# Scores by float32 products in four groups of 32 array columns, and outputs stored by accumulating transfers

## The chip, the core and the metric

The kernel runs on one core of one Trainium2 chip. The metric is the device time of one execution in microseconds; the median of three runs is given. The engines are TensorE (matmuls), VectorE, ScalarE, GpSimd and SP, which issues transfers. TensorE reads its weights and its moving operand from SBUF and writes PSUM; transfers run on 16 DMA engines, whichever engine issues them.

## What is computed

```python
q = cond @ Wq.T + bq                       # (2, 512), as 16 heads of 32
k = x @ Wk.T + bk;  v = x @ Wv.T + bv      # x: (2, 2048, 512)
scores = einsum('bhqd,bhkd->bhqk', q / sqrt(32), k)[:, :, 0, :]
attn = clip(scores, 0.0, 1.0)              # one weight per row of x and head
context = attn[..., None] * v
out = x + context.reshape(2, 2048, 512) @ Wo.T + bo
```

All is float32. There is one query per batch element, so the scores of a batch element are x times a 512x16 matrix `a` (Wk folded with the query), plus a constant `c`.

## The kernel before

**Layout.** x lies transposed (features on partitions) and is cut into four superblocks s = 0 to 3 of 1024 rows of x. Superblocks 0 and 1 belong to the first batch element, 2 and 3 to the second. A superblock is a 512x1024 matrix, in four quadrants Q11, Q12, Q21, Q22 of 256 features by 512 rows, each kept as 128 partitions x 1024 (two contraction tiles of 512 columns). One 512-KB transfer loads or stores a quadrant.

**Products.** Each of the two large products (values v, outputs) is a 2x2 block product done in the Strassen-Winograd way with 7 block products: the kinds B11, B21, B22 are quadrants of the operand and T1, T2, T3, T4 are sums of quadrants (T3 replaces Q12 in place). Each operand is split in two float32r parts: ScalarE's `hi` casts it to `form_hi`, VectorE's `lo` subtracts and writes `form_lo`. A block product is 12 matmuls of 128x512: high x high, high x low and low x high, for two contraction tiles and two output tiles. `done[kind]` counts them. ScalarE copies results out of PSUM (`copy_b11`, `copy_u2`, `copy_u3`, `copy_out21`), VectorE adds the rest (`add_out11`, `add_out22`, `add_out12`).

**Phases.** The work runs in phases, values and outputs of the superblocks in turn: V0 (by hand, the opening), V1, O0, V2, O1, V3, O2, O3. They are numbered 0 to 7. The order of every engine is written out by hand, call by call, and engines meet only at semaphores. Engines run in order, so a call that waits holds up all that stands behind it on its engine. `made(kind, phase)` counts an operand's versions.

**Scores.** For each superblock `scores(s, 0)` and `scores(s, 1)` multiply the quadrants' operands already split for the values with the weights `a_for_hi` and `a_for_lo`: 2 x 8 matmuls of 128x512. The first 64 array columns carry the high part of `a`, the other 64 the rest, each head in 4 copies. So ScalarE copies the result (`copy_scores`), SP swaps the halves of the partitions by two transfers (`swap_scores`), VectorE adds them (`sum_scores`), ScalarE applies bias and ReLU (`relu_scores`), and VectorE's `context` takes the minimum with 1 and multiplies by v. The score products hold `form_hi` of the kinds B11, B21, T3 and B22: the next `hi` of these waits for `score_done`.

**The weights of the scores** come up in the opening: `rows(q_rows...)` is four float32 matmuls of 32 columns x 512 rows into the partitions 0, 32, 64 and 96 on (line 453), then transposes, `scale_q`, `rows(a_rows...)`, ScalarE's `copy_a_rows`, transposes (`turn_score_weights`), VectorE's `fill_a`, `sum_c` and `split_a`.

**x and outputs.** x has one home, `x_raw`. A quadrant of the next superblock is loaded when its old operand has been split. Results of the outputs of superblocks 0 to 2 lie in `work[2]`. GpSimd adds x to them by an accumulating transfer from DRAM (`add_residual`, 12 transfers), and SP stores them afterwards (`store`). The last superblock adds x on VectorE (`add_x`) and is stored in pieces.

## Time and profile before

| what | value |
|---|---|
| median of 3 runs | 184.95 us (184.53 to 186.56) |
| the profiled execution's own time | 185.87 us |
| its span (first to last instruction) | 184.1 us |
| granted TensorE clock, mean | 1.00 |
| TensorE matmuls, busy | 178.1 us, 795 |
| VectorE, busy | 164.5 us, 175 |
| ScalarE, busy | 111.7 us, 150 |
| moved by DMA | 30.24 MB, mean 164 GB/s |

The span is what the page divides; the execution's own time holds 1.8 us more around it. Starts are counted from the span's start. The durations of neighbouring instructions of one engine overlap, above all those of matmuls, so the work of an engine is read from the distance between starts.

### The profile page before, as it was taken

The page shows a single profiled execution, that of the slowest core. Times are in us where ns is not written, and L with a number is a line of the kernel's source. Part 1 is how long each engine was busy: PE and PEld are TensorE (multiplying, and loading weights), DVE is VectorE, ACT ScalarE, POOL GpSimd, SP SyncE. Part 2 cuts the span into 40 slices and gives each one's busy share as a digit, 9 for nine tenths or more (in the row PEclk, how much of TensorE's full clock was granted, in tenths as well). Part 3 has the DMA queues.
Part 4 walks back from the last instruction along what each step waited for, and adds up shares of the span by engine and source line. Part 5 has one row for each costly group of instructions (what it writes and reads, how often), then busy time and mean ns, then how long its engine had stood idle before and what let it go on. Part 6 is the DMA issues. An engine that isn't in the chain of part 4 may idle for free.

```text
span 184.1 us, 2338 instructions
## 1 busy us (share of the span) xinstructions
PE 178.1 (97%) x795; PEld 143.1 (78%) x795; DVE 164.5 (89%) x175; ACT 111.7 (61%) x150; POOL 13.4 (7%) x18
## 2 busy tenths in 40 slices
PE   8999999999899999999999999999999999999990
PEld 2786767888688888888888888888888888878880
DVE  1798469999999997999999999999997999999851
ACT  3568394895776755575587567855466847493200
POOL 6000000000000020211000010121000010111000
PEclk9999999999999999999999999999999999999999
DMA  5999930049220226399788226399720216189786
GB/s 217 347 383 389 395 142 0 12 102 360 103 57 0 57 21 179 49 182 207 215 290 287 58 14 155 91 175 310 227 117 0 57 14 155 62 129 236 201 321 254
DMA packets 9355, 30.24 MB, mean 164 GB/s; under 512 B 1152, under 2 KB 1536, under 8 KB 9216
## 3 DMA queue, kind: packets, MB, share of 16 engines
q1 hardware_dynamic: 7616, 23.81, 35.5%
q0 software_dynamic: 1728, 6.29, 20.6%
q8 instruction: 6, 0.10, 0.2%
q14 instruction: 5, 0.04, 0.1%
HBM read 19.61 MB, written 8.39 MB: 152 GB/s over the span
## 4 chain that ended last, share of the span: by engine, by line
PE 81%; DMA 10%; DVE 3%; SPq 2%; issue 1%; ACT 1%; DVEq 0%
DMA x_raw<-x_t 10%; PE bank_y L350 9%; PE bank_y L352 9%; PE bank_y L354 9%; PE bank_x L350 8%; PE bank_x L354 8%; PE bank_x L352 8%; PE bank_z L354 6%; PE bank_z L352 6%; PE bank_z L350 6%; PE score_bank L412 4%; PE score_bank L413 4%; PE bank_z L467 1%; PE bank_z L466 1%; PE bank_z L465 1%
## 5 line engine op out<-in xcount | busy, mean ns | idle before, releaser
L576 ACT CAST form_hi<-work 128x1024 fp32r<-128x1024 f32 x28 | 29.1, 1051 | 20.8 <-PE score_bank L413 6.6
L832 DVE TENSOR_TENSOR form_lo<-work,form_hi 128x1024 fp32r<-128x1024 f32 (+1 forms) x30 | 35.1, 1185 | 0.9 <-ACT form_hi L576 0.9
L611 ACT ACTIVATE work<-bank_y,const 128x512 f32<-128x512 f32 x30 | 19.8, 686 | 7.9 <-PE bank_y L354 7.6
L817 POOL DMA_DIRECT2D work<-x_t x12 | 10.5, 876 | 153.6 <-DVE work L865 147.8
L350 PE MATMUL bank_x<-form_hi,wo_hi 128*128 128x512 f32 x52 | 20.3, 391 | 0.5 <-issue 0.5
L611 ACT ACTIVATE work<-bank_x,const 128x512 f32<-128x512 f32 x24 | 15.8, 685 | 8.2 <-PE bank_x L354 8.2
L352 PE MATMUL bank_x<-form_lo,wo_hi 128*128 128x512 f32 x52 | 20.2, 389 | 0.0
L354 PE MATMUL bank_x<-form_hi,wo_lo 128*128 128x512 f32 x52 | 20.2, 389 | 0.0
L854 DVE SCALAR_TENSOR_TENSOR work<-relu,work 128x1024 f32<-128x1024 f32 x16 | 19.3, 1220 | 0.3 <-ACT relu L640 0.3
L350 PE MATMUL bank_y<-form_hi,wv_hi 128*128 128x512 f32 x48 | 18.7, 389 | 0.0
L352 PE MATMUL bank_y<-form_lo,wv_hi 128*128 128x512 f32 x48 | 18.7, 389 | 0.0
L354 PE MATMUL bank_y<-form_hi,wv_lo 128*128 128x512 f32 x48 | 18.7, 389 | 0.0
L832 DVE TENSOR_TENSOR form_lo<-x_raw,form_hi 128x1024 fp32r<-128x1024 f32 x15 | 18.2, 1220 | 0.1
L576 ACT CAST form_hi<-x_sum 128x1024 fp32r<-128x1024 f32 x9 | 9.5, 1052 | 8.6 <-DVE x_sum L915 4.6
L865 DVE TENSOR_TENSOR work<-bank_z,work 128x1024 f32<-128x1024 f32 x12 | 14.6, 1218 | 0.0
L576 ACT CAST form_hi<-x_raw 128x1024 fp32r<-128x1024 f32 x12 | 12.5, 1048 | 2.8 <-PE bank_y L354 1.3
L832 DVE TENSOR_TENSOR form_lo<-x_sum,form_hi 128x1024 fp32r<-128x1024 f32 x9 | 11.0, 1220 | 2.1 <-ACT form_hi L576 2.1
L412 PE MATMUL score_bank<-form_hi,a_for_hi 128*128 128x512 f32 x32 | 12.6, 393 | 0.2 <-DVE a_for_hi L832 0.2
L413 PE MATMUL score_bank<-form_lo,a_for_lo 128*128 128x512 f32 x32 | 12.5, 389 | 0.0
L350 PEld LDWEIGHTS bank_x<-form_hi,wo_hi 128*128 128x128 f32 x52 | 9.8, 188 | 2.9 <-issue 0.9
L354 PEld LDWEIGHTS bank_x<-form_hi,wo_lo 128*128 128x128 f32 x52 | 9.8, 188 | 2.0
L352 PEld LDWEIGHTS bank_x<-form_lo,wo_hi 128*128 128x128 f32 x52 | 9.8, 188 | 2.0
(139 smaller groups left out, 375.9 us busy)
## 6 DMA issues: line engine op xcount, KB each, us to landing
x_raw<-x_t SPq DMA_DIRECT2D x16, 512.0 KB, 6.4
out_t<-work SPq DMA_DIRECT2D x14, 512.0 KB, 4.1
work<-x_t POOLq DMA_DIRECT2D x12, 512.0 KB, 5.5
score_others<-score_rows SPq DMA_DIRECT2D x16, 128.0 KB, 2.3
work<-first_t SPq DMA_DIRECT2D x2, 512.0 KB, 3.7
work<-wq_t SPq DMA_DIRECT2D x2, 512.0 KB, 8.8
work<-wk_t SPq DMA_DIRECT2D x2, 512.0 KB, 11.1
work<-wo_t SPq DMA_DIRECT2D x1, 1024.0 KB, 7.4
```

Of the source, the lines that this page charges most:

```text
L350: pe.matmul(bank[:, j, :], hi, form_hi[:, kind, k, :], start=k == 0 and not grows, stop=False, skip_group_check=grows)
L352: pe.matmul(bank[:, j, :], hi, form_lo[:, kind, k, :], start=False, stop=False, skip_group_check=grows)
L354: mm = pe.matmul(bank[:, j, :], lo, form_hi[:, kind, k, :], start=False, stop=k == 1, skip_group_check=grows)
L412: pe.matmul(bank, a_for_hi[:, b, at + k, :], form_hi[:, kind, k, :], start=first, stop=False)
L413: mm = pe.matmul(bank, a_for_lo[:, b, at + k, :], form_lo[:, kind, k, :], start=False, stop=last)
L465: pe.matmul(bank, hi, x_hi, start=k == 0 and not grows, stop=False, skip_group_check=grows)
L576: nc.scalar.copy(flat(form_hi, kind), raw(kind, phase)).then_inc(hi_ready[kind], 1)
L611: nc.scalar.activation(result_set(phase)[:, q, j * ROWS:(j + 1) * ROWS], of[:, j, :], ACT.Identity, bias=bias[:, tile:tile + 1], scale=sca ...
L817: pool.dma_start(output_set(s)[:, q, :], x_t[s, q], accum_op=ALU.add).then_inc(residual_added[q], 16)
L832: return nc.vector.tensor_tensor(to, of, hi.bitcast(F32), ALU.subtract)
L854: nc.vector.scalar_tensor_tensor(out=pair(context_set(s), q), in0=relu[:, half:half + 1, :].to_broadcast([P, 2, ROWS]), scalar=1.0, in1=pa ...
L865: nc.vector.tensor_tensor(to, bank[:, :, :], to, ALU.add).then_inc(semaphore, 1)
```

## The change

Three things change, and with them the written order of ScalarE and VectorE.

**Scores.** `scores(s)` reads x itself, unsplit, as float32. The 1024 rows of a superblock are four quarters of 256 rows, and each quarter goes to a group of 32 array columns of its own, that is to 32 partitions of the result: 16 matmuls of 32x256 a superblock (4 contraction tiles by 4 groups). The weights `a_copies` are plain float32, each head in 2 copies. Four ReLUs of 32x256 (`clip_scores`) bring the four groups beside each other on the first 32 partitions, and three transfers (`spread_scores`) copy these to the other partitions. The copy, the swap, the sum and the split of `a` with its zeros are gone. Since T3 stands where Q12 was, superblocks above 0 use `x_t3_ready` and a weight difference for Q22.

**x.** x has two homes, `x_homes[s % 2]`. Superblock 1 is loaded without waiting; superblock s waits for what used s - 2.

**Outputs.** SP copies x to the place of the output, DRAM to DRAM (`copy_x`, four transfers for each of superblocks 0 to 2), and GpSimd stores the results by accumulating transfers onto it.

```diff
-            def scores(s, half):
-                bank, b = score_bank[half][:, :], s // 2
-                wait(pe, score_copied, score_number(s, half) - 1)
...
-                for kind, at in parts:
-                    for k in range(2):
-                        first, last = (kind, k) == (parts[0][0], 0), (kind, k) == (parts[1][0], 1)
-                        pe.matmul(bank, a_for_hi[:, b, at + k, :], form_hi[:, kind, k, :], start=first, stop=False)
-                        mm = pe.matmul(bank, a_for_lo[:, b, at + k, :], form_lo[:, kind, k, :], start=False, stop=last)
+            def scores(s):
+                b = s // 2
+                pe.wait_ge(a_ready, b + 1)
+                for q in range(4):
+                    wait(pe, x_loaded[s % 2][q], loads(q, s))
+                if s > 0:
+                    pe.wait_ge(x_t3_ready, s)
+                wait(pe, clipped_ready, GROUPS * (s - 1))
+                for k in range(KT):
+                    for g in range(GROUPS):
+                        half, rows = g // 2, k % 2 * ROWS + g % 2 * QUARTER
...
+                        mm = pe.matmul(score_psum(s)[g * GROUP:(g + 1) * GROUP, :], a_copies[:, b, form, :], of,
+                                       start=k == 0, stop=k == KT - 1)
+                mm.then_inc(score_done, 1)
...
+            def clip_scores(s):
+                act.wait_ge(score_done, s + 1)
+                act.wait_ge(c_ready, 1)
+                if s > 0:
+                    for ready in context_ready:
+                        act.wait_ge(ready, s)
+                for g in range(GROUPS):
+                    at = slice(g * GROUP, (g + 1) * GROUP)
+                    nc.scalar.activation(relu[0:GROUP, g // 2, g % 2 * QUARTER:(g % 2 + 1) * QUARTER], score_psum(s)[at, :],
+                                         ACT.Relu, bias=c_score[at, b:b + 1]).then_inc(clipped_ready, 1)
...
+            def spread_scores(s):
+                sp.wait_ge(clipped_ready, GROUPS * (s + 1))
+                for g in range(1, GROUPS):
+                    sp.dma_start(relu[g * GROUP:(g + 1) * GROUP, :, :], relu[0:GROUP, :, :]).then_inc(relu_loaded, 16)
+            def copy_x(s):
+                for q in (Q11, Q22, Q21, Q12):
+                    sp.dma_start(out_t[s, q], x_t[s, q]).then_inc(x_copied[s][q], 16)
...
+            load_x(1, Q11)
+            load_x(1, Q12)
             sp.dma_start(wo_raw.rearrange("p t n -> p (t n)"), wo_t.rearrange("p b n -> p (b n)")).then_inc(wo_loaded, 16)
+            load_x(1, Q22)
+            load_x(1, Q21)
+            spread_scores(0)
+            next_x(2)
+            copy_x(0)
+            spread_scores(1)
+            next_x(3)
+            copy_x(1)
+            spread_scores(2)
+            copy_x(2)
+            spread_scores(3)
...
-            def add_residual(s, q, semaphore, count):
+            def store(s, q, semaphore, count):
                 pool.wait_ge(semaphore, count)
-                pool.dma_start(output_set(s)[:, q, :], x_t[s, q], accum_op=ALU.add).then_inc(residual_added[q], 16)
+                pool.wait_ge(x_copied[s][q], 16)
+                pool.dma_start(out_t[s, q], output_set(s)[:, q, :], accum_op=ALU.add).then_inc(accumulated[q], 16)
...
             first_values(Q21, banks[1], 2)
             copy_q_rows()
+            hi(B11, 1)
             hi(T1, 1)
-            first_values(Q12, banks[2], 4)
-            copy_a_rows()
             wo_part(W11, 0)
             wo_part(W12, 1)
             wo_part(W22, 3)
+            first_values(Q12, banks[2], 4)
+            copy_a_rows()
+            hi(B21, 1)
             hi(T2, 1)
```

TensorE at the end of the opening, before (the last products of V0, the first block of scores, then T1 of V1):

```order
L429 MATMUL bank_x<-form_hi,wv_lo 128x512 x4
L412 MATMUL score_bank<-form_hi,a_for_hi 128x512
L413 MATMUL score_bank<-form_lo,a_for_lo 128x512
L412 MATMUL score_bank<-form_hi,a_for_hi 128x512
L413 MATMUL score_bank<-form_lo,a_for_lo 128x512
L412 MATMUL score_bank<-form_hi,a_for_hi 128x512
L413 MATMUL score_bank<-form_lo,a_for_lo 128x512
L412 MATMUL score_bank<-form_hi,a_for_hi 128x512
L413 MATMUL score_bank<-form_lo,a_for_lo 128x512
L350 MATMUL bank_z<-form_hi,wv_hi 128x512
```

and the same place now:

```order
L412 MATMUL bank_x<-form_hi,wv_lo 128x512 x4
L395 MATMUL score_bank<-work,a_copies 32x256 x2
L395 MATMUL score_bank<-x_home,a_copies 32x256 x2
L395 MATMUL score_bank<-work,a_copies 32x256 x2
L395 MATMUL score_bank<-x_home,a_copies 32x256 x10
L327 MATMUL bank_z<-form_hi,wv_hi 128x512
```

Sixteen matmuls stand in one block where two blocks of eight stood, one on each side of T1; those of superblocks above 0 stand ahead of T2 of their values phase.

ScalarE in the opening, from `copy_q_rows` on, before (`wo_hi<-work2` are the three parts of Wo, the second COPY is `copy_a_rows`):

```order
L679 COPY relu<-score_bank0 128x512
L576 CAST form_hi<-x_sum 128x1024
L670 ACTIVATE work0<-bank_z,const 128x512 x2
L683 COPY relu<-score_bank0 128x512
L687 CAST wo_hi<-work2 128x512 x3
L576 CAST form_hi<-x_sum 128x1024
L660 CAST wv_hi<-work1 128x512
```

and now:

```order
L654 COPY relu<-score_bank0 128x512
L553 CAST form_hi<-x_home1 128x1024
L553 CAST form_hi<-x_sum 128x1024
L662 CAST wo_hi<-work2 128x512 x3
L645 ACTIVATE work0<-bank_z,const 128x512 x2
L658 COPY relu<-score_bank0 128x512
L553 CAST form_hi<-x_home1 128x1024
L553 CAST form_hi<-x_sum 128x1024
L635 CAST wv_hi<-work1 128x512
```

The casts of Wo moved ahead of `first_values(Q12)` and of `copy_a_rows`, and the first operands of superblock 1 moved in here.

VectorE in the same stretch, from `fill_a` to the last step of the scores' weights, before:

```order
L1030 TENSOR_REDUCE a_full<-score_bank1 128x128
L1033 TENSOR_TENSOR a_full<-a_full 128x64
L1052 TENSOR_REDUCE c_score<-score_bank0 128x2
L1045 CAST a_for_hi<-a_full 128x6x64
L1045 CAST a_for_lo<-a_full 128x6x64
L832 TENSOR_TENSOR a_for_hi<-a_full,a_for_hi 128x6x64
```

and now:

```order
L988 TENSOR_REDUCE a_full<-score_bank1 128x128
L991 TENSOR_TENSOR a_full<-a_full 128x64
L796 TENSOR_TENSOR wo_lo<-work2,wo_hi 128x512
L1003 TENSOR_REDUCE c_score<-score_bank0 128x2
L796 TENSOR_TENSOR form_lo<-x_home1,form_hi 128x1024
L997 COPY a_copies<-a_full 128x192
```

One copy stands for the split, with a part of Wo and `lo(B21,1)` ahead of it.

## Rows read from the trace of the kernel before

**Rows 1.** The page, part 1: busy us, share of the span, instructions.
```profile
PE 178.1 (97%) x795; PEld 143.1 (78%) x795; DVE 164.5 (89%) x175; ACT 111.7 (61%) x150; POOL 13.4 (7%) x18
```

**Rows 2.** The waits of TensorE: engine, line, releaser, total us, times, longest.
```profile
PE bank_x L350 <- issue: 0.5, 1, 0.5
```

**Rows 3.** Busy time by stretch; then clock, DMA share, GB/s.
```profile
120.00:160.00 40.00, 40.00 (x178) 33.13 (x177) 38.92 (x36) 23.92 (x31) 2.81 (x4) 1.00 0.49 128
```

**Rows 4.** The timeline of TensorE: start, us, engine, line, operation, count.
```profile
165.96 0.39 PE L350 MATMUL bank_x<-form_hi,wo_hi 128*128 128x512 f32 x1
...
168.68 0.39 PE L350 MATMUL bank_y<-form_hi,wo_hi 128*128 128x512 f32 x1
...
172.76 0.28 PE L465 MATMUL bank_z<-form_hi,wo_hi 128*128 128x256 f32 x1
172.87 0.28 PE L466 MATMUL bank_z<-form_lo,wo_hi 128*128 128x256 f32 x1
```

**Rows 5.** The timeline of VectorE from 46.8 us.
```profile
46.80 1.22 DVE L854 SCALAR_TENSOR_TENSOR work<-relu,work 128x1024 f32<-128x1024 f32 x1
47.93 0.68 DVE L841 TENSOR_TENSOR score_rows<-score_rows,score_others 128x512 f32<-128x512 f32 x1
48.53 0.69 DVE L832 TENSOR_TENSOR wo_lo<-work,wo_hi 128x512 fp32r<-128x512 f32 x1
```

**Rows 6.** Groups by form: count, then busy us and mean ns of one.
```profile
L412 PE MATMUL score_bank<-form_hi,a_for_hi 128*128 128x512 f32 x32 | 12.6, 393 | 0.2 <-DVE a_for_hi L832 0.2
...
L640 ACT ACTIVATE relu<-score_rows,c_score 128x512 f32<-128x512 f32 x8 | 5.8, 722 | 1.9 <-DVE score_rows L841 1.9
...
L630 ACT COPY score_rows<-score_bank 128x512 f32<-128x512 f32 x8 | 4.6, 575 | 0.0
```

**Rows 7.** The timeline of TensorE around the query rows (L453).
```profile
14.95 1.07 PE L429 MATMUL bank_y<-form_lo,wv_hi 128*128 128x512 f32 x4
15.95 1.06 PE L453 MATMUL score_bank<-work,const 128*32 128x512 f32 x8
16.95 0.73 PE L429 MATMUL bank_z<-form_hi,wv_hi 128*128 128x512 f32 x2
```

**Rows 8.** Line 453: duration in ns (min, median, max), first and last start.
```profile
L453 PEld LDWEIGHTS score_bank<-work,const x8: 106/108/109, 15.9 to 16.0; 128*32 128x32 f32 x8
L453 PE MATMUL score_bank<-work,const x8: 592/604/617, 15.9 to 16.4; 128*32 128x512 f32 x8
```

**Rows 9.** The timeline of ScalarE, then of TensorE, from 24.5 us.
```profile
24.52 0.59 ACT L683 COPY relu<-score_bank 128x512 f32<-128x512 f32 x1
24.99 1.68 ACT L687 CAST wo_hi<-work 128x512 fp32r<-128x512 f32 x3
...
26.06 0.28 PE L501 MATMUL score_bank<-bk_q,const 128*128 128x8 f32 x2
```

**Rows 10.** DMA issues (KB, median us to landing), and one of SP's timeline.
```profile
work<-x_t POOLq DMA_DIRECT2D x12, 512.0 KB, 5.5
work<-wo_t SPq DMA_DIRECT2D x1, 1024.0 KB, 7.4
...
16.91 0.43 SPq L285 DMA_DIRECT2D work<-wo_t  x1
```

**Rows 11.** The timeline of VectorE from 25.7 us.
```profile
25.71 1.23 DVE L930 TENSOR_TENSOR x_sum<-x_sum,x_raw 128x1024 f32<-128x1024 f32 x1 [0.99 <-DMA x_raw<-x_t]
...
28.60 0.68 DVE L1030 TENSOR_REDUCE a_full<-score_bank 128x128 f32<-128x512 f32 x1
...
29.57 0.36 DVE L1045 CAST a_for_hi<-a_full 128x384 fp32r<-128x384 f32 x1
```

**Rows 12.** The timeline of VectorE and TensorE around 50 us.
```profile
49.13 1.22 DVE L832 TENSOR_TENSOR form_lo<-work,form_hi 128x1024 fp32r<-128x1024 f32 x1
...
50.56 0.47 PE L350 MATMUL bank_x<-form_hi,wo_hi 128*128 128x512 f32 x1 [0.50 <-issue]
```

**Rows 13.** Stores of the output on SP: ns to issue, first and last start.
```profile
L325 SPq DMA_DIRECT2D out_t<-work x3: 588/686/710, 179.3 to 180.6; - x3
```

More of the change, by code:

```diff
@@ L561, in hi @@
                     semaphore, count = {
[L562 to L563 removed]
+                        B11: (x_loaded[s % 2][Q11], loads(Q11, s)), B21: (x_loaded[s % 2][Q21], loads(Q21, s)),
+                        B22: (x_loaded[s % 2][Q22], loads(Q22, s)),
                         T1: (x_t1_ready, s), T2: (x_t2_ready, s), T3: (x_t3_ready, s), T4: (x_t4_ready, s)}[kind]
@@ L569, in hi @@
                     act.wait_ge(semaphore, s + 1)
-                before, s_before = PHASES[phase - 1]
-                if before == VALUES and kind in FIRST_PHASE_KINDS and (kind != B22 or s_before == 0):
-                    act.wait_ge(score_done, score_number(s_before, kind in (T3, B22)) + 1)
+                if phase > 1 or kind not in FIRST_PHASE_KINDS:
+                    wait(act, done[kind], 2 * (phase - 1))
+                elif kind == T3:
+                    act.wait_ge(w21_done, 1)
                 else:
-                    wait(act, done[kind], 2 * (phase - 1))
+                    act.wait_ge(first_done, {B11: 2, B21: 4, B22: 8}[kind])
                 nc.scalar.copy(flat(form_hi, kind), raw(kind, phase)).then_inc(hi_ready[kind], 1)
@@ L1108, in _ @@
             fill_a()
+            wo_part(W12, 1)
             sum_c()
-            split_a(0)
-            wo_part(W12, 1)
+            lo(B21, 1)
+            copy_a(0)
             lo(T2, 1)
+            lo(T3, 1)
             wv_sum_part(S3, 3)
             x_t4(1)
+            lo(B22, 1)
             wo_sum(0)
+            lo(T4, 1)
             wo_sum(1)
-            lo(B11, 1)
-            lo(B21, 1)
-            lo(T4, 1)
             wo_sum(2)
-            lo(T3, 1)
+            wo_sum(3)
             wo_sum_part(S2, 1)
-            lo(B22, 1)
-            wo_sum(3)
-            sum_scores(0, 0)
             wo_sum_part(S1, 0)
+            wo_sum_part(S3, 2)
+            wo_part(W22, 3)
+            add_out11(1)
+            wo_sum_part(S4, 3)
+            copy_a(1)
             context(0, Q11)
-            add_out11(1)
-            context(0, Q21)
-            sum_scores(0, 1)
-            wo_sum_part(S3, 2)
+            context(0, Q12)
             lo(B11, 2)
-            context(0, Q12)
             context_t1(2)
             add_out22(1)
+            context(0, Q21)
             lo(T1, 2)
@@ L1179, in _ @@
             lo(B11, 5)
+            add_out12(3)
             lo(T3, 4)
-            add_out12(3)
+            add_out11(4)
             context_t4(4)
-            add_out11(4)
+            lo(B22, 4)
             lo(T4, 4)
-            lo(B22, 4)
             x_t1(5)
             lo(B21, 5)
-            x_t3(5)
             lo(T1, 5)
@@ L1230, in _ @@
             context_t2(7)
+            context(3, Q21)
+            lo(T2, 7)
+            lo(B21, 7)
             context_t3(7)
-            lo(T2, 7)
             context_t4(7)
```

327 lines of the change are left out of this document (117 added, 210 removed).

## The prediction, written before the changed kernel was run

> **What bounds the kernel now.** I read the page's busy shares first, then the waits by engine, then the busy time by stretch. The reader is to see that TensorE is busy 178.1 of 184.1 us [rows 1], that its longest wait is 0.5 us [rows 2], and that in a stretch such as 120 to 160 us it is busy all 40 us, with the granted clock at 1.00, the higher of its two levels (2.4 GHz) [rows 3]. VectorE stands close behind (38.9 of the 40 us). Busy shares of matmuls overlap, so I take the work from the distance between starts: twelve products from 165.96 to 168.68 us are 2.72 us, 0.2266 us for 512 columns, and a 256-column one is 0.119 us [rows 4]. VectorE's distances are 1.13 us for 128x1024 and 0.60 us for 128x512 [rows 5]. So the end is set by the number of matmuls, and what the change takes from TensorE comes off the span, if the other engines follow.
>
> **What goes from TensorE.** 64 score products, 32 with the high parts [rows 6] and 32 with the low, at 0.2266 us: **-14.5 us**.
>
> **What comes.** 64 float32 matmuls of 32 array columns by 256 rows, 16 per superblock. The trace has a near relative: the query rows, four float32 matmuls of 32 columns by 512 rows, written into four different groups of 32 columns, each with a moving operand of its own [rows 7, 8]. They are recorded as 8 matmuls, two passes each. The first start at 15.95 us, the last at 16.4 us, and each lasts 0.60 us: so the four groups run at the same time, and a pass over 512 rows takes 0.45 us, twice the 0.2266 us of an fp32r product. With 256 rows I take twice 0.119 = 0.233 us (rounding). A superblock has four contraction tiles of two passes, 8 rounds: 1.87 us. The switch costs extra on both sides: the product group ahead began at 14.95 us and four of its matmuls are 0.91 us, so without any switch the next would have begun at 15.86 us; two rounds of 0.45 us later would be 16.76 us, but the next group starts at 16.95 us and its first matmul is 0.11 us late because its weights load only then. That is 0.09 + 0.10 + 0.11 = 0.30 us. A block is then 2.17 us, four are **+8.7 us**. Both sides: below, 8 rounds with no switch, 1.8 us a block (7.2 in all); above, the weight loads stand open in each round (rival A), 3.0 us a block (12.1 in all). I take 8.7 because the row nearest to it is the same form of instruction.
>
> **The opening.** Here the new ScalarE order costs something. TensorE's rows of a need the copy of a_rows (L683); before it is finished at 25.1 us and TensorE turns to it at 26.06 us without a wait [rows 9]. After the change the three casts of wo stand ahead of first_values(Q12) and of that copy. They wait for wo_t, issued at 16.91 us, 7.4 us to landing: at 24.3 us, and at the latest at 24.99 us, where before they begin without a wait [rows 9, 10]. From 24.5 us: casts 1.65 us, two activations 1.15 us, copy 0.6 us, done at about 27.9 us. TensorE stands in front of its transposes for 1.8 us. It comes to scores(0) at 30.5 + 1.8 = 32.3 us, where they now start at 30.72 us after 0.2 us of waiting for the split of a [rows 6]: **+1.6 us** (from 0 if wo lands much earlier, to 2.1). VectorE's side is no later: x_t2(1) cannot start before x arrives at 25.7 us [rows 11], both before and after, since all loads go through one queue in nearly the same order; from its start at 25.7 us two sums and a wo part lead to fill_a at 28.60 us as before, the three small steps of fill_a and sum_c take 0.97 us [rows 11], and with one wo part more (0.60), lo(B21) (1.13) and the copy of a (0.3) a_ready comes at 31.6 us. This is hidden under the 32.3 us; should the ScalarE stall not come, a_ready is what is late next, at +0.9 us. What TensorE loses, VectorE does not: it fills idle time before 25.7 us (the last 1.0 us of it in this wait) with work that stood behind the scores (lo(B11,1) and lo(B21,1)), since home 1 lets x of superblock 1 in at once.
>
> **One wait goes.** The first output product (B11 of phase 2) starts at 50.56 us after an idle 0.50 us, and takes 0.47 us instead of 0.39, since lo(B11,2) ends only at 50.35 us [rows 12]. After the change that operand hangs on a shorter chain (below): walked through the order with these distances it is there at 48.8 us, for a product at 50.3 us: **-0.6 us**. If it were late, it would cost what it costs now.
>
> **The other engines, after the first block.** VectorE: eight sums of scores (0.60 each [rows 5]) and the split of a go; from copy_a(0) on the listing has 109 operations of 128x1024, 13 of 128x512 and small ones: 109 x 1.137 + 13 x 0.60 + 2.4 = 134 us, against TensorE's 576 x 0.2266 + 24 x 0.119 + 8.7 = 142 us of the same part. ScalarE: eight copies and eight ReLUs, 10.4 us busy, go [rows 6]; 16 clips of 32x256 come, a form that no row has. At the ReLU's 0.72 us each they would be 11.5 us, at half of it 5.8 us: from 1.1 us lost to 4.6 us gained, in an engine that is busy 61% [rows 1]; I take 0.5 us each and nothing either way. I followed the order row by row with these distances: the tightest place is T2 of each output phase, where B22's end, 0.2 us of release [rows 12], add_out12 (1.14) and lo(T2) (1.14) need 2.5 us while TensorE has B21, 2.7 us. It holds by 0.2 us. Everywhere else 1.5 us or more are left. TensorE's new waits for x_t3 before scores(2) and scores(3) are met 4 and 7 us early.
>
> **The score chain and SP.** Scores, four clips (2 us), three transfers of 128 KB (a single one of 512 KB takes 5.5 us to landing [rows 10]; I take 4). The context of superblock 0 has them at 40 us and wants them at 45 us. spread_scores(1) stands behind next_x(2) and the four copies of copy_x(0) on SP: 8 transfers of 0.5 MB, issued from about 37 us. Even at the 7.4 us that wo_t's 1 MB takes to landing in the full queue of the opening [rows 10] they are through at 67 us and the scores behind them at 71 us; the reader in VectorE comes at 76 us. The later ones have more room. GpSimd: its two memsets go, nobody waited for them; its accumulating transfers now write DRAM instead of SBUF. The nearest row is 5.5 us to landing; the results' home of superblock 0 is wanted again some 15 us after its last transfer was issued. Nothing for these, below nothing excluded since TensorE does not wait for them now.
>
> **The end.** The three last stores take SP 0.69 us each to issue, where wo_t's took 0.43 us [rows 10, 13]; behind the same queue stand the four stores of superblock 2 and the transfers that they wait for. These leave SP. I take **-0.3 us** (from 0 to -1).
>
> **Sum.** -14.5 + 8.7 + 1.6 - 0.6 - 0.3 = -5.1 us: span 179.0 us. The profiled execution took 185.87 us with a span of 184.1 us; it would become 180.8 us. The median of the runs shown is 184.95 us, 0.9 us under it: **179.9 us**.
>
> **Rivals.** *A, weight loads in the open.* A block has 32 weight loads of 0.108 us [rows 8]. If the four groups' next weights can't be loaded while their matmuls run, each round grows by 0.11 us to 0.34 us, with the switch 3.0 us a block: 12.1 instead of 8.7, 183.3 us. Against it: all eight loads of the query rows start between 15.9 and 16.0 us, the second pass's too, under the first pass's matmuls. For it: there are two sets of weights there, here eight.
> The Trainium skill, "TensorE: Matmul & The Clock Gate", section "The mechanism" of Part 3, says that weight loads overlap with matmuls in flight "only when row_grp differs"; here all groups use all rows, so by that rule rival A holds, and its 183.3 us. The rows named speak against it for the second pass and are silent on the third.
>
> *B, the followers slip.* TensorE's slack at T2 is 0.2 us per output phase, ScalarE's order is wholly new, and a conflict of two engines costs one operation, 0.6 to 1.1 us. Two to four of those: 182.5 us. Against it: VectorE has 8 us less to do than TensorE.
>
> *C, slower: TensorE is bound by issue in the blocks.* A block has 64 instructions in 2.17 us, 34 ns each. The shortest distance that the stream of weight load and matmul shows for 256 columns is 0.119 us a pair [rows 4]. If a pair cannot go faster, 32 pairs are 3.8 us, with the switch 4.1 us a block: 16.4 instead of 8.7, 187.6 us. It turns into a loss from 3.45 us a block on. Against it: the query rows' eight weight loads start within 0.1 us [rows 8].
>
> *D, slower too: accumulating into DRAM is slow.* The last four such transfers would be issued at about 143, 152, 157 and 161 us. If one takes 12 us and they run one by one, the last lands at 191 us: 192 us. It decides from 9 us each; now it is 5.5.
>
> *E, the change does not do what it says:* the groups run one after another, 16 matmuls of four times 0.119 us, 7.6 us a block, 202 us. The query rows exclude it as far as rows can.
>
> **How the numbers follow.** My forecast 60% (178 to 182), better than 178 us 7%, A 11%, B 11%, C 5%, D 3%, E and others 3%. A measurement of this kernel tells 1% from no change, 1.85 us: under 183.1 us is faster. Faster: 60 + 7, nearly all of B (9) and half of A (5), 81%. Same: the rest of A and B and a mild C, 10%. Slower: 9%. The range: below, blocks of 1.8 us, an opening of +0.9, an end of -1: -8.0, 177.0 us; above, A with the opening at +2.1 and nothing gained at the end: -0.9, 184.0 us. It leaves out C, D, E and a little of the rest.
>
> **What the profile after would show.** Score blocks of 2.1 to 2.3 us from start to the next product, with records that overlap by fours; TensorE idle 1.5 to 2 us before the transposes at about 28 us, waiting for ScalarE's copy; scores(0) at 32.3 us; hardly any other TensorE wait; the last matmul at about 174.6 us instead of 179.6; VectorE idle some 7 us more in waits for TensorE. I would be wrong if the blocks took 3 us or more, if TensorE waited for form_lo in many places, or if wo arrived before 22.5 us.

## The result and the profile after

| | before | changed |
|---|---|---|
| median of 6 runs each | 185.94 us (184.53 to 186.79) | 179.59 us (178.98 to 180.07) |
| the profiled execution's own time | 185.87 us | 178.98 us |
| its span | 184.1 us | 177.2 us |

The ratio is 0.967, with a 95% interval of 0.962 to 0.972: 3.3% faster. Forecast were 179.9 us (177.0 to 184.0). Single slow executions are left out of the ratios, here and below (the largest is 350.69 us, one of the six of `both_waits`). That 179.59 lies 0.3 us beside 179.9 is luck in part: the forecast took 5.1 us off a median of 184.95 us, while 6.4 us went off a median of 185.94 us. The span came out 1.8 us better than its sum, and the terms, some of which err against each other, say where.

The page, part 1, and the waits of TensorE after the change:

```profile
PE 172.3 (97%) x859; PEld 134.6 (76%) x859; DVE 158.2 (89%) x163; ACT 109.9 (62%) x150; POOL 10.7 (6%) x16
...
PE bank_z L454 <- PEq L1249: 0.8, 1, 0.8
PE bank_x L327 <- issue: 0.6, 1, 0.6
PE bank_y L327 <- ACT work L589: 0.5, 1, 0.5
```

Beside [rows 1, 2]: TensorE is still busy 97% of the span, 5.8 us less in all. The 0.8 us stand at the start, and stood there before. The wait of 0.5 us in front of B11 (then 50.56 us, [rows 12]) is gone, and two others have come.

**The blocks of scores and what is ahead of them.** TensorE's timeline, from its turn to the transposes of `a` to the first product behind `scores(0)`:

```profile
25.17 1.08 PE L412 MATMUL bank_x<-form_lo,wv_hi 128*128 128x512 f32 x4
26.09 0.28 PE L484 MATMUL score_bank<-bk_q,const 128*128 128x8 f32 x2
...
29.45 1.07 PE L412 MATMUL bank_x<-form_hi,wv_lo 128*128 128x512 f32 x4
30.45 0.41 PE L395 MATMUL score_bank<-work,a_copies 128*32 128x256 f32 x2
30.46 0.41 PE L395 MATMUL score_bank<-x_home,a_copies 128*32 128x256 f32 x2
30.69 0.39 PE L395 MATMUL score_bank<-work,a_copies 128*32 128x256 f32 x2
...
30.91 0.39 PE L395 MATMUL score_bank<-work,a_copies 128*32 128x256 f32 x2
...
31.12 0.39 PE L395 MATMUL score_bank<-work,a_copies 128*32 128x256 f32 x2
31.14 1.25 PE L395 MATMUL score_bank<-x_home,a_copies 128*32 128x256 f32 x18
32.31 0.50 PE L327 MATMUL bank_z<-form_hi,wv_hi 128*128 128x512 f32 x1
32.65 0.40 PE L329 MATMUL bank_z<-form_lo,wv_hi 128*128 128x512 f32 x1
```

Read by fours: two matmuls at 30.45 and two at 30.46 us are the first pass of the four groups, at 30.69 the next round starts, then 30.91 and 31.12: 0.22 us a round. The block lasts from 30.45 to 32.31 us, 1.86 us. That is 0.13 us more than eight rounds of 0.216 us, the length that `twice` (below) gives for a round: most of it lies between the start of the last pass and the first product behind it, 0.31 us. To either side the switch costs 0.09 us (30.45 is 1.00 us behind the start of a group of four that are worth 0.91) and 0.11 us (the first product needs 0.34 us to the next instead of 0.23). A block is 2.06 us; the other three are alike. In this execution there is no wait in front of the transposes or of `scores(0)`.

The weight loads of the blocks (the other 8 of the 128 read `work`), by line (ns: min, median, max; first and last start):

```profile
L395 PEld LDWEIGHTS score_bank<-x_home,a_copies x120: 106/110/110, 30.5 to 121.6; 128*32 128x32 f32 x120
```

Four loads of 0.11 us fall on each round of 0.22 us, so they overlap each other and the passes, and the round is not longer for them.

**The opening of ScalarE** (`wo_hi<-work` are the casts of Wo, L658 is `copy_a_rows`), and of SP the issue of wo_t:

```profile
22.39 1.66 ACT L662 CAST wo_hi<-work 128x512 fp32r<-128x512 f32 x3
...
25.11 0.58 ACT L658 COPY relu<-score_bank 128x512 f32<-128x512 f32 x1
...
7.03 0.43 SPq L276 DMA_DIRECT2D work<-wo_t  x1
```

wo_t is issued at 7.03 us and not at 16.91 [rows 10]. It then takes 15.3 us to landing and not 7.4, so 9.9 us at the issue become 2.0 us at the landing (22.3 us). Wo can be cast from 22.39 us, and the copy ends at 25.69 us, 0.4 us before TensorE comes.

**The two new waits.** The first stands at T2 of phase 2, at 59.8 us. ScalarE, VectorE and TensorE there:

```profile
55.30 1.94 ACT L615 ACTIVATE relu<-score_bank,c_score 32x256 f32<-32x256 f32 x4
57.26 2.00 ACT L553 CAST form_hi<-work 128x1024 fp32r<-128x1024 f32 x2
...
56.49 1.22 DVE L823 TENSOR_TENSOR work<-bank_z,work 128x1024 f32<-128x1024 f32 x1 [0.47 <-PE bank_z L331]
58.35 1.22 DVE L796 TENSOR_TENSOR form_lo<-work,form_hi 128x1024 fp32r<-128x1024 f32 x1 [0.63 <-ACT form_hi L553]
...
58.78 0.39 PE L331 MATMUL bank_y<-form_hi,wo_lo 128*128 128x512 f32 x1
59.78 0.47 PE L327 MATMUL bank_x<-form_hi,wo_hi 128*128 128x512 f32 x1 [0.61 <-issue]
```

1.00 us passes between the two starts instead of 0.227, and 0.31 to the next instead of 0.227: 0.85 us lost. The second stands at B21 of phase 4. Pieces of the chain that ended last (start, us, what):

```profile
91.26 1.23 DVE work L812
...
92.59 0.13 ACT relu L615
...
96.66 1.29 ACT work L589 x2
97.99 0.50 PE bank_y L327
```

`clip_scores(2)` (L615) writes the one `relu` that VectorE's `context` of superblock 1 (L812) still reads until 92.49 us; `copy_b11(4)`, `hi(B11,5)` and `copy_out21(3)` stand behind it, and the last of them lets TensorE go on: 0.78 us lost, counted in the same way. A third place, at 117.34 us, loses 0.24 us.

**The end.** The last addition of VectorE, the last issues of SP (a store of 256 KB and two of 128 KB), and a row of the DMA view (count, KB, us to landing):

```profile
174.33 0.42 DVE L931 TENSOR_TENSOR work<-score_bank,work 128x256 f32<-128x256 f32 x1 [0.29 <-PE score_bank L450]
...
173.62 1.50 SPq L302 DMA_DIRECT2D out_t<-work  x3
...
out_t<-work SPq DMA_DIRECT2D x2, 128.0 KB, 2.0
```

From 174.33 us to the span's end it is 2.8 us. Before, from VectorE's last addition at 179.93 us on, SP's last issues and the same row of the DMA view:

```profile
179.26 2.08 SPq L325 DMA_DIRECT2D out_t<-work  x3
...
out_t<-work SPq DMA_DIRECT2D x2, 128.0 KB, 3.0
```

That was 4.1 us. Of the 1.3 us between them 0.6 us lie before the end of SP's last issue (1.41 and 0.79 us behind the start of VectorE's last addition) and 0.7 us behind it, in the landing of the last piece (2.7 and 2.1 us).

### The profile page after: what moved, and what is told of

It is laid out like the page before. It is cut to its first block, busy times and chain, and to the rows that moved or that the text cites. A ratio compares the mean times of both kernels' runs of the same rounds, so it can differ in the third digit from the quotient of the medians.

```text
span 177.2 us, 2441 instructions
## 1 busy us (share of the span) xinstructions
PE 172.3 (97%) x859; PEld 134.6 (76%) x859; DVE 158.2 (89%) x163; ACT 109.9 (62%) x150; POOL 10.7 (6%) x16
## 4 chain that ended last, share of the span: by engine, by line
PE 90%; issue 4%; DVE 2%; ACT 2%; ACTq 0%; DVEq 0%
PE bank_y L327 9%; PE bank_y L329 9%; PE bank_y L331 9%; PE bank_x L327 8%; PE bank_x L329 8%; PE bank_x L331 8%; PE bank_z L327 5%; PE bank_z L329 5%; PE bank_z L331 5%; PE bank_x L412 5%; PE score_bank L395 4%; PE bank_z L412 3%; PE bank_z L454 2%; PE bank_x L430 2%; PE bank_y L430 2%
## 5 line engine op out<-in xcount | busy, mean ns | idle before, releaser
L589 ACT ACTIVATE work<-bank_x,const 128x512 f32<-128x512 f32 x24 | 15.8, 686 | 7.2 <-PE bank_x L331 7.1
L782 POOL DMA_DIRECT2D out_t<-work x12 | 10.5, 875 | 151.9 <-DVE work L823 142.6
L812 DVE SCALAR_TENSOR_TENSOR work<-relu,work 128x1024 f32<-128x1024 f32 x16 | 19.2, 1218 | 0.0
L796 DVE TENSOR_TENSOR form_lo<-x_home,form_hi 128x1024 fp32r<-128x1024 f32 x15 | 18.3, 1220 | 0.8 <-ACT form_hi L620 0.8
L553 ACT CAST form_hi<-x_home 128x1024 fp32r<-128x1024 f32 x12 | 12.6, 1052 | 0.4 <-PE bank_y L331 0.3
L327 PE MATMUL bank_y<-form_hi,wo_hi 128*128 128x512 f32 x28 | 11.0, 394 | 0.5 <-ACT work L589 0.5
L327 PEld LDWEIGHTS bank_y<-form_hi,wv_hi 128*128 128x128 f32 x48 | 9.0, 188 | 3.0 <-issue 1.2
## 6 DMA issues: line engine op xcount, KB each, us to landing
work<-wo_t SPq DMA_DIRECT2D x1, 1024.0 KB, 15.3
```

Of the source, the lines that this page charges most:

```text
L327: pe.matmul(bank[:, j, :], hi, form_hi[:, kind, k, :], start=k == 0 and not grows, stop=False, skip_group_check=grows)
L553: nc.scalar.copy(flat(form_hi, kind), raw(kind, phase)).then_inc(hi_ready[kind], 1)
L589: nc.scalar.activation(result_set(phase)[:, q, j * ROWS:(j + 1) * ROWS], of[:, j, :], ACT.Identity, bias=bias[:, tile:tile + 1], scale=sca ...
L782: pool.dma_start(out_t[s, q], output_set(s)[:, q, :], accum_op=ALU.add).then_inc(accumulated[q], 16)
L796: return nc.vector.tensor_tensor(to, of, hi.bitcast(F32), ALU.subtract)
L812: nc.vector.scalar_tensor_tensor(out=pair(context_set(s), q), in0=relu[:, half:half + 1, :].to_broadcast([P, 2, ROWS]), scalar=1.0, in1=pa ...
```

## Experiments

All ratios are to the kernel before, run on the same chip beside them.

### The two parts alone

`scores_only` is the changed kernel with the old way of the outputs (add_residual on GpSimd, stores on SP); `outputs_only` is the kernel before with the new one. The edit of `outputs_only`; `scores_only` has it the other way round:

```diff
-            def store(s, q):
-                sp.wait_ge(residual_added[q], 16 * (s + 1))
-                sp.dma_start(out_t[s, q], output_set(s)[:, q, :]).then_inc(stored[q], 16)
+            def copy_x(s):
+                for q in (Q11, Q22, Q21, Q12):
+                    sp.dma_start(out_t[s, q], x_t[s, q]).then_inc(x_copied[s][q], 16)
...
-                pool.dma_start(output_set(s)[:, q, :], x_t[s, q], accum_op=ALU.add).then_inc(residual_added[q], 16)
+                pool.wait_ge(x_copied[s][q], 16)
+                pool.dma_start(out_t[s, q], output_set(s)[:, q, :], accum_op=ALU.add).then_inc(accumulated[q], 16)
```

> The changed kernel with the outputs the old way: x added to the results by the accumulating transfer into SBUF, then a plain store by SP, and no copy of x to the outputs. Theory: the new stores give only the shorter end (last VectorE sum to the end of the span 2.9 us instead of 4.2), so this is 0.5 to 1.3 us slower than the changed kernel: 5.0 to 5.7 us faster than before (ratio 0.969 to 0.973), with the last matmul at the same 174 us. Rival: the new stores carry several us through transfers that get out of the way of the loads; then TensorE would show new waits and the ratio be above 0.98. Second rival: the end is shorter because the core ends earlier in general, not by the stores; then there is no difference.

> The kernel before with only the outputs changed: copies of x from DRAM to DRAM and accumulating stores onto them. Theory: only the end is shorter: 0.5 to 1.3 us faster than before (ratio 0.993 to 0.997), matmuls at the same times. Rival: no change, or slower since the copies crowd the loads of x and the swaps of scores (ratio 1.00 to 1.01).

**Measured.** `scores_only` 180.2 us, ratio 0.970 (0.965 to 0.974), span 179.3 us; `outputs_only` 183.9 us, 0.990 (0.985 to 0.994), span 182.0 us. `scores_only` came as expected; `outputs_only` gained more than the 0.3 to 0.7% of its theory, with an interval that reaches down to 0.6%. From VectorE's last addition to the span's end it is 3.9 us in `scores_only` (from 175.40 us on) and 2.8 us in `outputs_only` (from 179.25 us on); both match the way in which each stores its outputs. The scores carry 5.6 us of the gain. For the outputs the times give between 0.6 us (180.2 against 179.6 us, within the intervals) and 2.0 us (0.0105 of 185.75), the ends of the profiles 1.1 us (3.9 against 2.8) and 1.4 us (4.1 against 2.8). The span of `scores_only` is 2.1 us over that of the changed kernel: 1.1 us is the end, and 1.1 us the opening, which the edit does not touch (`scores(0)` at 31.51 us). More on that below.

### What a round costs: each block twice

```diff
-                for k in range(KT):
+                for k in [*range(KT), *range(KT)]:
```

> The changed kernel with every block of score matmuls made twice (the second restarts the sums, so the result is the same): 64 float32 matmuls more. Theory: a round of four groups by 256 rows is about 0.22 to 0.23 us and TensorE sets the end, so 8 rounds more in each of four blocks add 7.0 to 7.4 us to the changed kernel: ratio to before 1.00 to 1.01. Rival: there is slack on TensorE or the other engines set the end, and it adds 4 us or less.

**Measured.** 186.6 us, ratio 1.005 (1.002 to 1.009): 7.2 us over the changed kernel (0.0388 of 185.75 us). The second half of the first block starts at 32.79 us and the block ends at 34.63 us:

```profile
32.79 0.39 PE L395 MATMUL score_bank<-work,a_copies 128*32 128x256 f32 x2
...
34.63 0.50 PE L327 MATMUL bank_z<-form_hi,wv_hi 128*128 128x512 f32 x1
```

Eight more rounds are 3.59 - 1.86 = 1.73 us, 0.216 us each. From the first score matmul to the start of the last matmul the profile has 150.45 us, the changed kernel 143.56 us: 6.89 us more, four times 1.73 us being 6.91. What a block costs is on TensorE's path to its full length.

### The order inside a block

`group_by_group` gives a group all its eight passes in a row; `two_tiles` gives each group four, then each the other four:

```diff
-                for k in range(KT):
-                    for g in range(GROUPS):
+                for g in range(GROUPS):                                      # group_by_group
+                    for k in range(KT):
...
+                for k2 in range(0, KT, 2):                                   # two_tiles
+                    for g, k in [(g, k) for g in range(GROUPS) for k in (k2, k2 + 1)]:
```

> The changed kernel with the two loops of a score block exchanged: all four contraction tiles of one column group, then the next group, so that neighbouring matmuls meet in the same 32 columns. Theory: only matmuls of different groups run at the same time, so a block takes 16 matmuls of about 0.46 us, 7.5 us instead of 1.9: the four blocks add 20 to 23 us, ratio 1.08 to 1.09. Rival: the engine looks far enough ahead to overlap the groups whatever their order, and the time stays; a half-way result (an overlap only where groups change) gives 6.3 us a block, 16 to 18 us.

**Measured.** 190.5 us, ratio 1.025 (1.020 to 1.029): 10.8 us over the changed kernel, about half of what was expected of one group after another. TensorE's timeline of the first block:

```profile
31.41 1.05 PE L395 MATMUL score_bank<-work,a_copies 128*32 128x256 f32 x4
32.30 0.38 PE L395 MATMUL score_bank<-x_home,a_copies 128*32 128x256 f32 x1
32.30 0.40 PE L395 MATMUL score_bank<-work,a_copies 128*32 128x256 f32 x1
32.51 0.38 PE L395 MATMUL score_bank<-x_home,a_copies 128*32 128x256 f32 x1
32.54 0.38 PE L395 MATMUL score_bank<-work,a_copies 128*32 128x256 f32 x1
...
35.93 0.50 PE L327 MATMUL bank_z<-form_hi,wv_hi 128*128 128x512 f32 x1
```

Tiles 0 and 1 of the groups 0 and 1 come from `work`, tiles 2 and 3 from `x_home`. The four passes over `work` from 31.41 us are group 0's; from 32.30 us its passes over `x_home` run in step with passes over `work`, which can only be group 1's, though these stand behind all eight of group 0 in the program. So a group begins when the one ahead has four passes left, 0.89 us after it began: 3 x 0.89 + 8 x 0.216 = 4.4 us, and with the 0.13 us that a block of the changed kernel has beside its rounds 4.54, against 4.52 measured. From this I made a theory, that a group takes up to four passes ahead, and tested it:

> The changed kernel with another order of the same 64 instructions of a block: two contraction tiles (four passes) of group 0, then of groups 1, 2 and 3, then the other two tiles in the same way. With all of a group's eight passes in a row (group_by_group) a block took 4.52 us, and the first pass of group 1 started at 32.30 us, beside the fifth of group 0's eight. Theory (a column group takes up to four passes of its own in advance; only a fifth holds up what stands behind it for other groups): here no group ever gets more than four in a row, so all four groups run side by side; a block takes 1.9 to 2.1 us, and the ratio is that of the changed kernel, 0.967 to 0.970. Rival (only two groups run side by side when an order is not group after group in each round): 3.5 to 4.5 us a block, 6 to 10 us more in all, ratio 1.00 to 1.02.

**Measured.** The first block lasts from 31.13 to 33.03 us, 1.90 us, the others 1.90 to 1.91 us. 180.2 us, ratio 0.973 (0.966 to 0.980), where 0.967 to 0.970 was expected; in the profile it is 143.92 us from the first score matmul to the start of the last matmul, 0.36 us over the changed kernel, of which the four blocks are 0.15 us. Within 0.04 us the first passes of all four groups start, though three more passes of each of the groups 0 to 2 stand ahead of group 3's in the program: so the passes that wait do so for each group apart, and not in one row of three for all. Group after group in every round is not needed; four passes of one group in a row do no harm. Five to seven were not tried.

### The two new waits

From here on the profiles are compared by the time from the first score matmul to the start of the last matmul, since the opening of the profiled executions differs by up to 1.2 us though it is the same in ten of the kernels (`scores(0)` at 30.28 to 31.51 us). The changed kernel has 174.01 - 30.45 = 143.56 us.

```diff
             # t2_first, VectorE
-            add_out12(1)
             lo(T2, 2)
+            add_out12(1)
...
             # clip_later, ScalarE
-            clip_scores(2)
             copy_b11(4)
             hi(B11, 5)
             copy_out21(3)
+            clip_scores(2)
```

> The changed kernel with one line moved on VectorE: in phase 2 the operand of T2 (lo(T2,2)) stands ahead of add_out12(1), the addition of the values of the superblock before. In the changed kernel TensorE waits 0.61 us in front of T2 of phase 2 at 59.8 us, with the slow first product behind it 0.85 us in all. Theory (the wait is VectorE's order: end of B22, then add_out12(1) 1.14 us, then the operand 1.14 us, against TensorE's 2.7 us of B21): the operand is ready 1.1 us earlier, the wait at 59.8 us is gone, span 177.2 - 0.85 = 176.4 us, ratio to the kernel before about 0.962. Rival 1 (it comes back: what reads the result of add_out12(1), or the bank that it frees, is then late by 1.1 us): a wait of 0.5 to 1 us stands somewhere in the next 3 us and the ratio stays at 0.966. Rival 2 (the operand waits for ScalarE's hi part, not for VectorE): the wait at 59.8 us stays as it is, ratio 0.967.

> The changed kernel with one line moved on ScalarE: clip_scores(2) stands behind copy_out21(3) instead of three calls ahead of it. In the changed kernel TensorE waits 0.51 us in front of B21 of phase 4 at 98.0 us for copy_out21(3), with the slow first product 0.78 us; ScalarE stood 1.3 us in front of clip_scores(2), since the single home of the ReLU's results was still read by VectorE's context of superblock 1. Theory (that wait held the three calls behind it): the wait at 98.0 us is gone, span 177.2 - 0.78 = 176.4 us, ratio about 0.962; the scores of superblock 2 reach their reader about 2 us later, which has more than that in hand. Rival 1 (the clip is late for its reader): VectorE waits in context of superblock 2 and TensorE for an output operand behind it, ratio 0.967 or more. Rival 2 (ScalarE was late for other reasons than the clip): TensorE's wait at 98 us stays above 0.3 us.

> The changed kernel with both moves: lo(T2,2) ahead of add_out12(1) on VectorE, clip_scores(2) behind copy_out21(3) on ScalarE. If each of the two waits was only the cost of its place in an order, they add up: TensorE has only the 0.24 us wait at 117 us left after the opening, the last matmul starts at 174.01 - 0.85 - 0.78 = 172.4 us, span 175.6 us, ratio about 0.958. If one takes up the slack that hid the other, less than the sum: 0.960 to 0.963. If VectorE (busy 89%) becomes the bound in their place, 0.966.

**Measured.** `t2_first`: ratio 0.971 (0.967 to 0.976), 143.59 us, and the wait stayed as it was. Rival 2 holds. VectorE now stands 2.3 us, and ScalarE shows why:

```profile
58.63 1.23 DVE L796 TENSOR_TENSOR form_lo<-work,form_hi 128x1024 fp32r<-128x1024 f32 x1 [2.32 <-ACT form_hi L553]
...
55.58 1.94 ACT L615 ACTIVATE relu<-score_bank,c_score 32x256 f32<-32x256 f32 x4
57.55 2.00 ACT L553 CAST form_hi<-work 128x1024 fp32r<-128x1024 f32 x2
...
60.07 0.47 PE L327 MATMUL bank_x<-form_hi,wo_hi 128*128 128x512 f32 x1 [0.61 <-issue]
```

`hi(T2,2)` stands behind `clip_scores(1)`; its input was there at 56.2 us. `clip_later`: ratio 0.968 (0.964 to 0.972), 143.13 us. The wait at 98 us is gone, but the 0.78 us gave only 0.43: TensorE now loses 0.3 us at 111.8 us, where VectorE has worked without a pause since 104.8 us. `both_waits`: 0.969 (0.964 to 0.974), 143.06 us. The sum expected did not come, since one of its two halves aimed at the wrong engine.

So the other block of clips was moved too (`clips_later`), and with it `lo(T2,2)` (`all_waits`):

```diff
             # ScalarE; clip_scores(2) as above
-            clip_scores(1)
             hi(T2, 2)
+            clip_scores(1)
```

> The changed kernel with two of the blocks of clips moved on ScalarE: clip_scores(1) behind hi(T2,2) (before: ahead of it) and clip_scores(2) behind copy_out21(3). With lo(T2,2) ahead of add_out12(1) the wait in front of T2 of phase 2 stayed at 0.61 us, VectorE standing 2.3 us for the high part of T2; that high part starts on ScalarE at 57.26 us as the clips end, though its input was there at 56.0 us. New theory (the clips hold both): the wait at 60 us is gone but for 0 to 0.2 us, since VectorE still has add_out12(1) in front; from the first score matmul to the start of the last matmul 143.1 us (clip_scores(2) moved alone) becomes 142.4 us. Counted so, because the opening of the profiled executions differs by 0.75 us. Ratio to the kernel before 0.962 to 0.966. Rival (VectorE is now the one that is late, at 105 to 119 us it works without a pause and TensorE waits there 0.2 us twice): what is won at 60 us is lost before 120 us, 143.0 us.

> Both blocks of clips moved as in the run beside it, and lo(T2,2) ahead of add_out12(1) on VectorE. Theory: no wait at 60 us at all, 142.3 us from the first score matmul to the start of the last; ratio 0.962 to 0.965. Rival (VectorE is the bound at 105 to 119 us): 143.0 us, and the ratio of the changed kernel, 0.967.

**Measured.** `clips_later` 178.4 us, ratio 0.963 (0.960 to 0.967), 142.38 us where 142.4 was expected, with 0.13 us left of the 0.85 at 60 us; the rival with its 143.0 us fell. `all_waits` 178.1 us, ratio 0.961 (0.958 to 0.965), 142.23 us, span 175.7 us. That is 1.33 us less than the changed kernel between the two fixed points; the intervals of the two ratios overlap (the changed kernel has 0.962 to 0.972). `lo(T2,2)` ahead of `add_out12(1)`, worth nothing in `t2_first`, gave the last 0.15 us of it. T2 of phase 2 in `all_waits`, ScalarE and TensorE:

```profile
55.89 1.05 ACT L553 CAST form_hi<-work 128x1024 fp32r<-128x1024 f32 x1 [0.66 <-DVE work L858]
56.84 1.94 ACT L615 ACTIVATE relu<-score_bank,c_score 32x256 f32<-32x256 f32 x4
...
58.61 0.39 PE L331 MATMUL bank_y<-form_hi,wo_lo 128*128 128x512 f32 x1
58.84 0.39 PE L327 MATMUL bank_x<-form_hi,wo_hi 128*128 128x512 f32 x1
```

### The opening, with the old times of the loads

`late_loads` puts the old waits back ahead of the loads of superblock 1 on SP, and so ahead of wo's; `late_loads_act` also puts ScalarE's `first_values(Q12)` and `copy_a_rows` back ahead of the casts of Wo:

```diff
             # SP, both
+            for n in (0, 2):
+                sp.wait_ge(wv_sum_ready[n], 1)
+            for form in second_w:
+                sp.wait_ge(wv_lo_ready[form], 1)
+            sp.wait_ge(lo_ready[B11], 1)
             load_x(1, Q11)
+            sp.wait_ge(lo_ready[T3], 1)
             load_x(1, Q12)
...
             # ScalarE, late_loads_act
+            first_values(Q12, banks[2], 4)
+            copy_a_rows()
             wo_part(W11, 0)
             wo_part(W12, 1)
             wo_part(W22, 3)
-            first_values(Q12, banks[2], 4)
-            copy_a_rows()
```

> The changed kernel with the loads of superblock 1 held back on SP by the waits that they had before (the sums of Wv, the split operands of superblock 0), which stand ahead of wo's load too: wo_t is issued at about 17 us instead of 7.0. This restores the times on which the prediction's +1.6 us for the opening rested. Theory (the step failed because wo arrived 1.9 us earlier than reckoned, the order of ScalarE is as I said): wo's casts start at 24.3 to 25 us on ScalarE instead of 22.4, the copy of a_rows ends at 27.5 to 28 us instead of 25.7, TensorE stands 1.5 to 2.2 us in front of the transposes of a, scores(0) starts at 32 to 32.6 us and the span is 1.2 to 1.9 us longer, ratio 0.974 to 0.980. Rival (the casts of Wo were never on the path, a_ready is set by VectorE): less than 0.5 us of wait, scores(0) at 31 to 31.6, ratio 0.969 to 0.973.

> The same late loads, and on ScalarE first_values(Q12) and the copy of a_rows ahead of the three casts of Wo, as in the kernel before. Theory: the wait in front of the transposes is gone; scores(0) then starts at 30.7 to 31.6 us, set by VectorE (x of superblock 1 arrives at 25.7 us), ratio 0.967 to 0.972, 0.5 to 1.5 us better than the run beside it. Rival (late loads cost by themselves, by VectorE standing for x): no better than the run beside it.

**Measured.** `late_loads` 180.4 us, ratio 0.972 (0.968 to 0.977). Its opening on ScalarE, then SP and TensorE:

```profile
23.77 1.66 ACT L670 CAST wo_hi<-work 128x512 fp32r<-128x512 f32 x3 [0.46 <-DMA work<-wo_t]
...
26.49 0.58 ACT L666 COPY relu<-score_bank 128x512 f32<-128x512 f32 x1
...
17.15 0.43 SPq L282 DMA_DIRECT2D work<-wo_t  x1
...
25.61 1.08 PE L420 MATMUL bank_x<-form_lo,wv_hi 128*128 128x512 f32 x4
27.22 0.36 PE L492 MATMUL score_bank<-bk_q,const 128*128 128x8 f32 x2 [0.53 <-ACT relu L666]
```

ScalarE waits for wo_t, its copy ends at 27.07 us, and TensorE stands in front of the transposes: 1.61 us between the two starts instead of 0.92, 0.69 us lost, where 1.5 to 2.2 were expected. wo took 6.6 us from issue to the cast, not 7.4, and TensorE came 0.44 us later.

But this does not show that the old issue time costs anything. In `scores_only`, where wo_t is issued at 7.76 us, the same wait stands at the same place:

```profile
23.61 1.66 ACT L664 CAST wo_hi<-work 128x512 fp32r<-128x512 f32 x3
...
27.05 0.36 PE L486 MATMUL score_bank<-bk_q,const 128*128 128x8 f32 x2 [0.52 <-ACT relu L660]
```

In each of the ten profiles with the opening of the changed kernel wo_t is issued at 7.0 to 8.0 us, takes 14.9 to 15.8 us to landing, and its casts start within 0.1 us of that. With casts from 22.2 to 22.4 us on TensorE loses nothing in front of the transposes, at 22.86 us 0.15 us (`t2_first`), at 23.2 us 0.25 to 0.35 (`twice`, `clip_later`, `two_tiles`), at 23.5 to 23.6 us 0.68 (`group_by_group`, `scores_only`); in `both_waits`, where TensorE itself comes 0.7 us later, nothing at 22.97. So the wait depends on when wo_t arrives, six of the ten have it, and the changed kernel's profile is one of the four without. What delays the queue in one execution and not in another is not shown. In `late_loads_act` (180.2 us, 0.974, 0.969 to 0.978) that wait is gone, and 0.46 us stand in front of `scores(0)`, at 31.16 us, because VectorE's x of superblock 1 comes late (its copy of `a` starts at 30.80 us instead of 29.63). The two can't be told apart by time, but by place. Between the two fixed points they have 143.59 and 143.60 us, as the changed kernel has.

## Why the prediction came out as it did

**Bound, right.** From `scores(0)` to the start of the last matmul TensorE took 148.89 us before (179.61 - 30.72) and 143.56 us after, 5.33 us less: -14.5 (64 products) + 8.25 (four blocks of 2.06) - 0.85 (waits that went, at 50.56 us, forecast as -0.6, and one of 0.1 us at 163 us) + 1.87 (0.85 + 0.78 + 0.24) = -5.2 us. That TensorE's longest wait before was 0.5 us was misread: 0.8 us stand at its start, in both kernels, and nothing hangs on them.

**The blocks, right and a little too dear.** +8.7 was forecast, 8.25 came: a round is 0.216 and not 0.233 us. The switch was right: 0.09 us ahead of the block, 0.13 at its end and 0.11 at the first product are 0.33 us, for 0.30. Rival A fell: a round did not grow by a weight load, though eight sets of weights follow each other. The Trainium skill, "TensorE: Matmul & The Clock Gate", "The mechanism" of Part 3, would have loads overlap only between row groups; here all groups use all rows, and the trace speaks against it for groups of columns. Rival C fell: 64 instructions in 1.86 us are 29 ns each, where the limit that it took from pairs of full width was 59; and the query rows need 0.45 us for a round of as many instructions on twice the rows [rows 7, 8], so a round goes by its rows and not by its issue. Rival E, that the groups would run one by one, decides by order: with all eight passes of a group in a row a block costs 4.52 us (not the 7.6 of the rival), with four in a row 1.90.

**The opening, the step that failed.** "They wait for wo_t, issued at 16.91 us, 7.4 us to landing: at 24.3 us" took the issue time from the trace of before, while the waits of SP that held it there belong to what the change removes. I had used that removal for x in the same paragraph and not for wo, which stands behind it in the same queue. Issued at 7.03 us instead of 16.91, wo_t let the casts start at 22.39 us, before the 22.5 us that the prediction itself gave as a sign that it was wrong, and there was no stall: -0.27 (`scores(0)` at 30.45 instead of 30.72 us) against +1.6. The mechanism, ScalarE's casts ahead of `copy_a_rows`, is there: six of ten profiles with this opening lose 0.15 to 0.7 us by it. Over the ten `scores(0)` starts at 31.0 us on average, so against 30.72 us this term is nearer to +0.3 than to -0.27; against the 30.38 us of `outputs_only`, the other profile with the old opening, it is +0.6. That the profiled execution, the fastest of the six, has none of it is luck, and goes the way of the difference between 6.9 us by the spans and 6.4 us by the medians. With the old issue time (`late_loads`) it was 0.7 us and not 1.6. "a_ready is what is late next" held in `late_loads_act`, with 0.46 us for 0.9. That x_t2(1) "cannot start before x arrives at 25.7 us", both before and after, was wrong for the same reason: it started at 24.09 us (`scores_only`: 25.30).

**ScalarE at nothing, wrong by 1.6 us.** A clip takes 0.47 us, four in a row 1.94 us, close to the 0.5 taken; the total of ScalarE was right (109.9 us busy for 111.7). But the total is not what costs: two of the four blocks of clips stand ahead of an operation that TensorE needs within 2 us. Rival B's size was right for two places. The place named as tightest, T2 of an output phase, is where one of them fell, but not through add_out12 and lo(T2): `t2_first` took that chain away and gained nothing. The second place has a further cause, the one home of the ReLU's results: ScalarE stood 1.3 us in front of the clips until `context` had read it. Without both, 1.33 of the 1.63 us came back (`all_waits`); the rest went to a wait of 0.3 us at 110.1 us.

**The end, right in sign, too small.** -0.3 was forecast (from 0 to -1), -1.3 came. I priced SP's issuing alone, and at half of the 0.6 us that it gave. The last pieces also land sooner, 2.0 instead of 3.0 us with their issue, 0.7 us without it, once the twelve stores of SP are gone.

**Rival D** fell: an accumulating transfer onto DRAM takes 5.1 us to landing, into SBUF it took 5.5 [rows 10].

The sum for the two profiled executions, then: -14.5 + 8.25 - 0.85 + 1.87 - 0.27 - 1.3 = -6.8 us, against -6.9 measured and -5.1 forecast. The opening (1.9 us), the end (1.0), the blocks (0.4) and the waits that went (0.3) were forecast too dear, the new waits (1.9) too cheap: half of the 3.6 us cancelled by luck.

## What to carry to other kernels

When a change takes a wait out of a queue, move every issue behind it to its new time, before pricing anything that hangs on one of them. A batch of small operations (here four of 0.47 us) on an engine that is only 62% busy can still cost what it takes beyond the slack at its place, here 0.8 of 1.94 us twice, if it stands ahead of a link that the busiest engine wants next; put it behind that link, and look for the place by who waits for the operation behind the batch. Where the opening of a profiled execution varies as much as the effect (here 1.2 us), compare from one fixed instruction to another, and read a term of the opening from several executions.

## What was not expected of the hardware

Float32 matmuls of 32 columns in four different column groups run side by side, each on a moving operand of its own, at 0.216 us a pass of 256 rows for all four, with four weight loads of 0.11 us hidden in each round. And the groups do not keep the order of the program among each other: a group starts while four passes of the one before it are still to come, so that eight passes in a row per group cost 4.52 us a block and four in a row 1.90 us. That it is a depth of four is the reading that fits both orders; it was not measured with other counts.
